# Cross-attention of a two-layer decoder on one core: the scores of three units ahead are issued behind the turn of a unit's exponentials instead of ahead of it

## The reference, cut to what matters

```python
q = proj(query, Wq, bq)
k = proj(key, Wk, bk)
v = proj(value, Wv, bv)
attn = jnp.einsum('bhqd,bhkd->bhqk', q, k) / jnp.sqrt(jnp.float32(Dh))
attn = jax.nn.softmax(attn, axis=-1)
out = jnp.einsum('bhqk,bhkd->bhqd', attn, v)
out = out.transpose(0, 2, 1, 3).reshape(B, -1, D)
out = jnp.einsum('bsd,ed->bse', out, Wo) + bo
```

## Time and profile before

| | |
|---|---|
| three runs, median | 757.38 us (755.39 to 758.69) |
| profiled execution, its own time | 756.76 us |
| span of the profiled execution, first to last instruction | 755.0 us |
| cross-attention stage in it, from the first scores to the first matmul of the quantised network | 465.8 to 600.6 us |
| mean granted clock of TensorE | 0.986 |

### The profile page before, as it was taken

One profiled execution on the slowest core, in us unless ns is written; L12 is line 12 of the kernel. 1 busy time (PEld: TensorE's weight loads), 2 busy tenths in 40 slices (PEclk: granted clock), 3 DMA queues, 4 the chain that ended last, 5 costly groups with the idle time before them and its releaser, 6 DMA issues.

```text
span 755.0 us, 11075 instructions
## 1 busy us (share of the span) xinstructions
PE 704.1 (93%) x3942; PEld 392.9 (52%) x3942; DVE 493.1 (65%) x1179; ACT 547.2 (72%) x998; POOL 160.0 (21%) x224
## 2 busy tenths in 40 slices
PE   8999999989999999999999999879998899992897
PEld 6642222212222226889888886544555644441686
DVE  3895656745313316486547566849977877988786
ACT  3569999999999994664042345789886533899991
POOL 3641233201010001114153241333221100000022
PEclk9999999999999999999999999999999999997899
DMA  8132213041345250302426000001100000000002
GB/s 238 63 43 43 29 29 94 19 85 36 91 119 162 50 165 10 112 11 102 137 87 223 1 1 2 0 31 54 44 0 1 2 1 0 0 1 0 0 29 83
DMA packets 56973, 41.48 MB, mean 55 GB/s; under 512 B 37106, under 2 KB 53720, under 8 KB 56792
## 3 DMA queue, kind: packets, MB, share of 16 engines
q1 hardware_dynamic: 56216, 40.13, 19.5%
q10 hardware_dynamic: 704, 0.66, 0.3%
HBM read 27.94 MB, written 4.46 MB: 43 GB/s over the span
## 4 chain that ended last, share of the span: by engine, by line
PE 48%; ACT 29%; DVE 13%; issue 8%; POOL 2%; POOLq 0%; DVEq 0%; ACTq 0%
ACT arena L683 18%; PE banks L2281 8%; PE banks L2043 7%; PE banks L2059 6%; PE banks L1714 4%; PE banks L1700 3%; ACT arena L808 2%; PE banks L1904 2%; DVE arena L1539 2%; PE banks L2171 2%; PE banks L1684 1%; DVE arena L1068 1%; PE banks L2073 1%; DVE arena L1076 1%; PE banks L1939 1%
## 5 line engine op out<-in xcount | busy, mean ns | idle before, releaser
L683 ACT ACTIVATE arena<-banks 128x1024 f32<-128x1024 f32 x256 | 235.4, 1163 | 0.1
L1714 PE MATMUL banks<-arena 128*32 128x512 f32 x1024 | 136.4, 604 | 0.8 <-DVE arena L1153 0.4
L1700 PE MATMUL banks<-arena 64*128 64x512 f16 x512 | 83.2, 383 | 4.4 <-ACT arena L683 1.2
L2281 PE MATMUL banks<-arena 128*128 128x512 f32 x192 | 83.0, 593 | 0.2 <-ACT arena L866 0.2
L1700 PEld LDWEIGHTS banks<-arena 64*128 64x128 f16 x512 | 20.0, 93 | 103.5 <-ACT arena L683 94.2
L808 ACT ACTIVATE arena<-banks,arena 128x77 f32<-128x77 f32 x256 | 64.6, 374 | 12.5 <-DVE arena L1429 12.5
L432 POOL TENSOR_SCALAR arena<-arena 128x2 f32<-128x2 f32 (+2 forms) x39 | 11.7, 301 | 259.2 <-DVE arena L1071 259.2
L764 ACT ACTIVATE arena<-banks,arena 128x256 f32<-128x256 f32 x64 | 26.9, 471 | 49.3 <-PE banks L2043 49.3
L2281 PEld LDWEIGHTS banks<-arena 128*128 128x128 f32 x192 | 36.2, 190 | 46.3 <-issue 42.6
L2059 PE MATMUL banks<-arena 128*128 128x256 f32 x256 | 56.5, 380 | 1.2 <-ACT arena L705 1.2
L2043 PE MATMUL banks<-arena 128*128 128x256 f32 x256 | 56.2, 379 | 0.0
(11 more groups left out here) (268 smaller groups left out, 1231.7 us busy)
## 6 DMA issues: line engine op xcount, KB each, us to landing
arena<-in_L_ffn_w SPq DMA_DIRECT2D x16, 1024.0 KB, 7.4
w_kept<-arena SPq DMA_DIRECT2D x3, 768.0 KB, 3.6
arena<-w_kept SPq DMA_DIRECT2D x3, 768.0 KB, 4.4
arena<-in_x SPq DMA_DIRECT2D x3, 512.0 KB, 8.0
out_x<-arena SPq DMA_DIRECT2D x3, 512.0 KB, 2.9
arena<-in_L_ffn_b SPq DMA_DIRECT2D x1, 1024.0 KB, 11.5
arena<-in_L_ffn_w_gate SPq DMA_DIRECT2D x1, 768.0 KB, 6.6
arena<-in_L_ffn_w_up SPq DMA_DIRECT2D x1, 768.0 KB, 8.4
```

What stands on the lines that cost most here:

```text
L683: act.activation(PT[(TB * u + kt) % 3][:, half], PS[:, 2 * (n % 3):2 * (n % 3) + 2, :], ACT.Exp, scale=DH ** -0.5 / QK_UP ** 2).then_inc(s ...
L1700: mm = pe.matmul(bank(2 * (n % 3) + h), KT[u % 2][64 * h:64 * h + 64, P * kt:P * kt + P], QT[u % 2][64 * h:64 * h + 64, 512 * half:512 * h ...
L1714: mm = pe.matmul(PS[32 * j:32 * j + 32, 6, :], VS[w][:, kt, h, :], PT[(TB * u + kt) % 3][:, half, h, :], start=(kt == 0), stop=(kt == TB - 1))
L2281: mm = pe.matmul(bank(2 + n % 4), (wgT if n < IC * G4 else wuT)[:, k, P * c:P * c + P], XT[:, k, 512 * g:512 * g + 512], start=(k == 0), s ...
```

## The change

In step n of TensorE's loop the scores of unit n+3 are issued behind the turn of unit n, and so, in steps 4, 12 and 20, behind the queries too. No other stream changes.

```diff
@@ -2222,11 +2222,11 @@
             output(7, range(1, TE))
             for n in range(1, UX):
                 g, m = n // 8, n % 8
-                if n + AHEAD < UX:
-                    xa_scores(n + AHEAD)
                 if m == 4 and g + 1 < G4:
                     queries(g + 1)
                 p_turn(n)
+                if n + AHEAD < UX:
+                    xa_scores(n + AHEAD)
                 if n == 2:
                     pe.wait_ge(sem("proj_y"), 3)
                     x_group_turn("ln_c", E, CONV_N[3], 3, b0=6)
```

## The result

The changed kernel took 768.97 us (median of 4 runs, 766.14 to 772.53) beside 757.85 for the kernel before on the same chip: ratio 1.015, interval 1.0129 to 1.0172. It is slower by 11.1 us. I had forecast 764.6 with a range up to 768.0: the sign was right, the size was not, and the measured time lies 1 us outside the range.

A forecast was written before the change was run, and what follows sets the result against it. No engine is full in the cross-attention stage; a handshake among three in-order queues (TensorE, ScalarE, VectorE) bounds it. Step costs sum to 7.2: 756.8 + 7.2 = 764.0, forecast as 764.6 against the median 757.38; range 760.5 to 768.0.

The forecast's parts named there:

- S(n+3) can always start one copy earlier than T(n): Cross-attention stage: scores (S) need earlier exponentials, the turn (T) the copy behind them; scores lay hidden under that copy.
- n=1 to 3, nothing: First moved units: minimums wait for VectorE's own work, not the scores; no cost, up to 0.8 us each if uncovered.
- n=4, 8, 12, 16, 20, 21 to 24, 27 and 28: Steps of TensorE's loop where later scores delay exponentials: +0.9, +0.65, +2.75, +0.75, +0.9, +0.65 and +0.6 us.
- The collision repeats: Step 12: VectorE's affine (L1387) again runs beside POOL's L548, one operation taking 2.57 us; without it the sum is 5.2.
- The turns gain nothing: Turns up to 0.72 us earlier where TensorE is late; the next exponentials still wait for the minimum, so counted as nothing.
- rival D: Faster: where TensorE is late, the earlier turn brings copy and exponentials forward 0.72 us; 753.8, chance 0.04.
- I keep both and count no new one: TensorE's two falls to 1.2 GHz in the stage, 1.7 us each, stay; no further fall added to the sum.
- rival B: Longer gaps let TensorE's clock fall once or twice more: +1.7 to +3.4 us, 766.3 to 768; chance 0.17.
- The wait of L808: ScalarE's exponentials waiting for the VectorE minimum (L1429): to grow from 12.5 to near 18 us.
- The signs: What the profile after should show: changed waits, E(7) (exponentials of unit 7) 0.9 late, E(16) about 4.3, parallel traces from E(31).
- the order's 7.2: Sum in us of all step costs from issuing scores behind turns and queries, with no new clock fall; chance 0.50.

The follow-up runs named there:

- e1: Kernel before with scores behind the turn in steps 4, 12 and 20 only, so behind the queries; 762.5 us, ratio 1.0073.
- e2: Kernel before with scores behind the turn in all steps but 4, 12 and 20; 760.81 us, ratio 1.0046.
- e3: Kernel after with GpSimd's bias of group 2 (L548) moved from step 12 to step 13; 764.62 us, ratio 1.0099.
- e6: Kernel before with GpSimd's bias of group 2 (L548) one step later; 756.88 us, ratio 0.999.
- e8: Kernel before with GpSimd's bias of group 2 one step later and extra unread scores in steps 4 and 26; 756.24 us, ratio 0.998.
- e9: Kernel after with idle time filled by extra unread scores and GpSimd's bias of group 2 one step later; 763.56 us, ratio 1.0087.
- e5: Kernel before with scores behind the turn in steps 10, 17, 18, 22 and 28 only, where TensorE is late; 757.72 us, ratio 1.0006.
- e4: Kernel after with nine extra, overwritten calls of scores where TensorE waits ahead of the turn or queries; 765.26 us, ratio 1.0109.
- e7: Kernel before with scores of step 4 computed twice and of step 26 three times, filling TensorE's idle time; 755.62 us, ratio 0.9977.

## Why the prediction was right or wrong

- *S(n+3) can always start one copy earlier than T(n), so moving it behind exposes it.* Right. L2129 stopped waiting for L808, L2144 waits 11.8 us for L820.
- *n=1 to 3, nothing.* Right: E(1) to E(6) keep their places to 0.01 us against E(0).
- *n=4, 8, 12, 16, 20, 21 to 24, 27 and 28.* The orders' parts are right to 0.25 us each, and their sum 0.4 too low. e1 and e2 show that 21 to 24 holds only with the rest in place.
- *The collision repeats.* Right (3.76 us again), and e3 shows it is the cause of 2.1 of the 2.75 us of step 12, which cost 0.6 without it where I had 0.9. The expectation from "SBUF — State Buffer" in the Trainium skill, section "Who interferes with whom", agrees with all twelve profiles: one operation of 2.57 to 2.58 us in the eight in which L548 runs beside the affine, and 0.51 at most in e3, e6, e8 and e9, where it doesn't.
- *The turns gain nothing.* Right, by e5. The 1.8 us at n=28, which I counted for rival D, were an effect of the clock's fall.
- **TensorE's clock: "I keep both and count no new one".** This is the step that failed. Its parts were wrong both ways: the fall at the queries of step 4 did not come back (-1.70), and three other ones, one of them double, came (+4.66 where they met work on the path). Net +2.96 in the profile, where I had 0; e4, with all but one fall gone from its profile, was 3.7 faster in the median (3.1 by the ratios). I had the places (ahead of T(6), T(16) and the queries of n=20: all three fell), and the price of 1.7 each, but treated them as a rival B of 0.17, because the kernel before held its clock over a gap of 1.30. The case doesn't show when such a gap brings a fall and when not, so the number of falls could not be worked out from my rows; but no net fall at all was the term put at nothing with the least reason.
- The wait of L808 rose to 24.7, not 18. The clock has little part in that, since e4 still has 23.3: I had added up only the waits that lengthen the path, and part of the rest is traded against the wait for the turn, as in e5.
- *The signs.* L2129's wait, L2144's wait, the long L1387 and the parallel traces from E(31) to the end of the stage (21.3 us in both) came as written; behind the stage the new trace is 1.6 us longer. E(7) was to start 0.9 late and started 0.79 early, and E(16) was to be 4.3 late and was 2.7 late, both by the missing fall of step 4. By E(7) alone I would have called the mechanism wrong; the runs without a fall in that place show that it isn't: from E(0), E(7) is 0.9 and E(16) 4.3 later in e4 than in e7.
- The range ended at 768.0: 757.4, the order's 7.2 and two falls of 1.7. The measured 768.97 stands beside 757.85 for the kernel before, 0.5 higher than the time I added to. The order took 0.4 more than forecast, the net falls in the profile 0.4 less than B's two. That leaves 0.6 that the stage doesn't explain; the longer part behind it, 1.6 us in the profile, may be its source, which isn't shown.

## What to carry to other kernels

In a hand-written order, put first what can start first: an operation whose inputs are ready one step earlier fills a wait, and behind an operation that waits it costs up to its own length (0.7 to 0.9 us a step here for scores of 0.79) and what its consumers' queues add. Follow the consumer's queue, not only the consumer: a late operand costs most where its reader stands ahead of other work (step 12 cost three times step 4). A change that leaves TensorE idle in new places must be priced with the clock in the sum and not beside it, and one profile of it is one draw among several.

## What the runs showed of the hardware

- The clock's fall doesn't follow from the length of the single gap ahead of it. The queries of step 4 ran at 2.4 GHz behind 2.30 us of idle time in the kernel after, and at 1.2 GHz behind 1.30 and 0.83 us with scores between them in the kernel before; those of step 20 ran at 1.2 GHz behind 2.23 us in the kernel after and at 2.4 GHz behind 2.21 us in e3.
- A fall costs 1.7 us where it meets back-to-back matmuls (queries 3.70 to 5.40), and nothing by E(13) where another engine is last (500.5 in the kernel after).
- Matmuls whose result nobody reads can pay for themselves: one call of scores more in step 4 and two in step 26 (where e7 also has the real scores behind the turn) gave 1.6 us.
- The profiled executions of e3 and e8 entered the stage 3 us later than the others (468.7 and 469.0 beside 465.3 to 467.1); each had a stretch at 1.2 GHz early on (at 56.0 and 12.1 us). That may be part of why single executions of this kernel spread by several us; it wasn't tested.
